# Shifted-window attention and a Fourier layer on one core: the clamp of the square sums on GpSimd, and the second normalisation written back to PSUM

## The chip, the cores and the metric

The kernel runs on one NeuronCore of a Trainium2 chip. A core has TensorE (matrix products, results in PSUM), VectorE, ScalarE (functions such as exp, log, gelu), GpSimd, and SyncE, which here only issues transfers. Each engine runs its own list of instructions in order; they are tied together by semaphores that an instruction raises when it is done and on which others wait. In the profile the engines are PE, DVE, ACT, POOL and SP; PEld is TensorE's weight load, and a name with a q is the engine's sequencer. The metric is the device time of one execution in microseconds (us).

## The reference

The input is an image batch x of shape (8, 256, 256, 64), float32. Two layers follow one another.

Layer 0 is a shifted-window transformer block. The image is cut into windows of 4x4 positions (a shift by 8 in both directions maps windows to windows). In each window, q, k and v are projections of x, with 4 heads of 16 channels:

```
qn = q / max(norm(q), 1e-12)          # likewise kn
attn = softmax(qn @ kn.T * scale + bias + mask)
x = x + layernorm(proj(attn @ v)) * g1 + b1
x = x + layernorm(fc2(gelu(fc1(x)))) * g2 + b2
```

The norms are over the 16 channels of a head; this is where the square sums and their clamp come from: max(sum of squares, 1e-24) is the square of the clamped norm. The layer norms are over the 64 channels.

Layer 1 subtracts a moving average of 25 along one axis, mixes the first 128 Fourier modes with complex matrices, one per channel, and adds the average back. It is linear and is done here as one 256x256 matrix per channel.

## The kernel before, in words

There are three stages. A short one (to about 262 us) forms constants and the 64 channel matrices. The long one, to about 6770 us, is layer 0. The last one, the Fourier layer, multiplies by the channel matrices and writes the output; it contains none of the code that is changed.

The long stage works on 512 groups. A group is 4 image rows over the full width: 64 windows, 1024 positions, laid out as 128 partitions (2 halves of the image's width x 64 channels) x 512 columns, or, turned, as 128 positions x 8 slots x channels. It is a software pipeline written out by hand: in every step each engine does one piece of work for groups of different age. In the code a group d steps old is called `i`d: `project_qk(i1)` is the projection of the group that came in one step ago, `gain2(i10)` the end of the second layer norm of the group that came in ten steps ago. The order of the calls at the end of each `step` is the engine's order. 16 steps are written out ahead of the loop and 10 behind it. The loop of TensorE unrolls 2 steps, ScalarE's 4, those of VectorE, GpSimd and SyncE 8. `need(engine, semaphore, group)` makes the engine wait for that group's piece; `before(g)` is the group that came in one step earlier.

The orders of one step, with the lines of the profile's rows:

- VectorE: regroup_x i1 (L855), normed1 i8 (L918), add1 i8 (L927), turn_prob i5 (L912), normed2 i10 (L933), gain2 i10 (L939), sum_squares i2 (L861), clamp i2 (L867), bias i4 (L884), maximum i4 (L893), turn_k i3 (L873), turn_q i3 (L879), qk_out i1 (L840), v_out i1 (L849), sum_prob i4 (L899), invert i4 (L906).
- TensorE: first_layer i9 in two halves (L595), weighted i6 (L551), scores i4 (L531), turn_x i0 (L492), project i7 (L563), second_layer i9 in two halves (L607), project_qk i1 (L502), project_v i1 (L512), variances i7 and i9 (L579, L583).
- ScalarE: keep_o i6 (L698), gelu i9 (L730), square1 i7 (L704), gelu i9 (L730), keep_x i0 (L674), a table load (L737), square2 i9 (L710), log_norm i2 (L679), root_norm i2 (L686), exponent i4 (L692), log_norms i7, i9 (L716), root_norms (L724), a table load (L744).
- GpSimd: divide i5 (L1042), square i2 (L997), expand_v i5 (L1004, two instructions), add2 i10 (L1053), shift i4 (L1036), scale_norm i2 (L1012), norm_k i2 (L1018), norm_q i2 (L1027).
- SyncE issues the transfers: store of y (L377), load of x (L341), copies of x and x1 (L346, L351), swap of halves (L364), spread_p (L358), spread_k (L371). spread_p and spread_k are four transfers each into `rows`, which TensorE's L551 and L531 read.

PSUM has eight banks of 128x512 float32. MA (banks 0, 1) and MB (2, 3) serve the projections and the first layer by turns, so that L595 waits until L840 has copied MA out. Banks 4 and 5 serve the scores (SB) and weighted sums (PV), the variances (VV) and the turned input (XT) by turns. D1 (bank 6) holds the attention's projection, H2 (bank 7) the second layer's output. normed1 writes its result back into D1; normed2 writes its result to a buffer in SBUF, `dn2`.

The clamp's chain: GpSimd squares (square), VectorE sums 16 at a time to 128x64 (sum_squares, into `ss`) and clamps (into `ssc`), ScalarE takes the log and from it the inverse root, GpSimd multiplies q and k by it.

Of the kernel before, what the change touches and what calls it, by code (L numbers as in the profile page):

```python
# [83 lines left out]
def swin_then_fourier(nc, x, qkv_wt, qkv_b, v_b, proj_wt, proj_b, logit_scale, cpb_w1t, cpb_b1, cpb_w2t,  # L84
# [11 lines left out]
    with ExitStack() as ctx:  # L96
# [11 lines left out]
        def carve(cols):  # L108
            a = used[0]
            used[0] += cols  # L110
            assert used[0] <= 2 * T * C
            return arena[:, a:a + cols]
# [41 lines left out]
        pT = carve(512)  # L154
        vexp = carve(1024).rearrange("p (s h e d) -> p s h e d", s=SLOTS, h=HEADS, e=2)
        oT = [carve(512) for _ in range(2)]
        sq1, sq1x, sq2, dn2, yg = (carve(512) for _ in range(5))
        x1T, x1r = [carve(512) for _ in range(2)], [carve(512) for _ in range(4)]
        l12, r12 = (carve(1024).rearrange("p (k n) -> p k n", k=2) for _ in range(2))
        ystripe = [sb(f"ystripe{i}", ROWS * HALF)[:, :].rearrange("p (r n) -> p r n", r=ROWS)  # L160
# [61 lines left out]
        def there(g):  # L222

            return not isinstance(g.base, int) or 0 <= g.base + g.off < G

        def need(eng, s, g, per=1):

            if there(g):
                assert isinstance(g.base, int) or PEEL + g.off >= 0
                eng.wait_ge(s, g.base * per + (g.off + 1) * per)  # L230
# [13 lines left out]
        def settled(eng):  # L244

            eng.sem_inc(passed, 1)

        def before(g, n=1):
            return Group(g.base, g.off - n)
# [176 lines left out]
        def _(pe):  # L426
# [57 lines left out]
            def step(s, k):  # L484
# [114 lines left out]
                def second_layer(g, kk, done):  # L599
                    if there(g):  # L600
                        if kk == 0:
                            need(pe, gelu0, g)
                            need(pe, dn2_sb, before(g))
                        else:
                            need(pe, gelu1, g)
                        for a in range(2):
                            ins = mm(H2[a * C:a * C + C, :], w2[:, kk, :], hT[kk][:, a, :],  # L607
                                     start=(kk == 0), stop=(kk == 1), tile_position=(0, a * C))
                        ins.then_inc(done, 1)
# [163 lines left out]
        def _(dve):  # L773
# [59 lines left out]
            def step(s, k):  # L833
# [24 lines left out]
                def sum_squares(g):  # L858
                    if there(g):
                        need(dve, squared, g)  # L860
                        dve.tensor_reduce(ss, sq.rearrange("p (n d) -> p n d", d=HD), AX.X, ALU.add).then_inc(summed, 1)  # L861

                def clamp(g):
                    if there(g):
                        need(dve, summed, g)
                        need(dve, logged, before(g, 2))
                        ts(ssc[ring(g, 2)], ss, 1e-24, None, ALU.max).then_inc(clamped, 1)  # L867

                def turn_k(g):
                    if there(g):  # L870
# [58 lines left out]
                def normed2(g):  # L929
                    if there(g):  # L930
                        need_norms(dve, r12_sb, i8, i10)
                        need(dve, yg_sb, before(g))
                        stt(dn2, H2, be2, r12[:, 1, :], ALU.add, ALU.mult).then_inc(dn2_sb, 1)  # L933

                def gain2(g):
                    if there(g):
                        need(dve, dn2_sb, g)
                        need(dve, y_sb, before(g))
                        ts(yg, dn2, g2, o12, ALU.mult, ALU.add).then_inc(yg_sb, 1)  # L939

                regroup_x(i1)
                normed1(i8)
# [2 lines left out]
                normed2(i10)  # L945
                gain2(i10)
                sum_squares(i2)
                clamp(i2)
                bias(i4)
                maximum(i4)  # L950
                turn_k(i3)
# [24 lines left out]
        @block.gpsimd  # L976
        def _(pool):
            tt = pool.tensor_tensor
            pool.memset(ident, 0.0).then_inc(made_id, 1)
            pool.wait_ge(made_id, 1)  # L980
            pool.affine_select(out=ident, in_=ident, compare_op=ALU.not_equal, fill=1.0, base=0,
                               pattern=[[-1, P]], channel_multiplier=1).then_inc(made_id, 1)
            pool.memset(qe, 0.0).then_inc(made_id, 1)
            pool.memset(rows[:, :], 0.0).then_inc(made_id, 1)
            pool.wait_ge(made_id, 4)
            pool.wait_ge(consts, consts_in)
            pool.wait_ge(set_up, 15)

            def step(s, k):
                i0, i1, i2, i3, i4, i5, i6, i7, i8, i9, i10, i11 = ago(s, k)  # L990

                def square(g):
                    if there(g):
                        need(pool, qk_sb, g)
                        need(pool, summed, before(g))
                        q = qk[ring(g, 2)].rearrange("p w s n -> p (w s n)")
                        tt(sq, q, q, ALU.mult).then_inc(squared, 1)  # L997

                def expand_v(g):
                    if there(g):  # L1000
                        need(pool, vb_sb, g)
                        need(pool, pv_ps, before(g))
                        for e, done in ((0, v0_sb), (1, v1_sb)):
                            tt(vexp.rearrange("p s h e d -> p (s h) e d")[:, :, e, :],  # L1004
                               vb[ring(g, 4)].rearrange("p (n d) -> p n d", d=HD),
                               par[:, e:e + 1].unsqueeze(2).to_broadcast([P, 32, HD]), ALU.mult).then_inc(done, 1)

                def scale_norm(g):
                    if there(g):
                        need(pool, rooted, g)  # L1010
                        r = rn[ring(g, 2)][:, 0]
                        tt(r, r, scale.unsqueeze(1).to_broadcast([P, SLOTS, HEADS]), ALU.mult).then_inc(scaled, 1)  # L1012

                def norm_k(g):
                    if there(g):
                        need(pool, rooted, g)
                        need(pool, kT_sb, before(g))
                        tt(kn.rearrange("p (n d) -> p n d", d=HD),  # L1018
                           qk[ring(g, 2)][:, 1].rearrange("p s (h d) -> p (s h) d", d=HD),
                           rn[ring(g, 2)][:, 1].rearrange("p s h -> p (s h)").unsqueeze(2).to_broadcast([P, 32, HD]),  # L1020
                           ALU.mult).then_inc(kn_sb, 1)

                def norm_q(g):
                    if there(g):
                        need(pool, scaled, g)
                        need(pool, qT_sb, before(g))
                        tt(bass.AP(tensor=qe.tensor, offset=qe.offset, ap=[qe.ap[0], [64, 16], [48, 2], [1, HD]]),  # L1027
                           qk[ring(g, 2)][:, 0].rearrange("p s (q h d) -> p (s q) h d", q=2, h=2),
                           rn[ring(g, 2)][:, 0].rearrange("p s (q h) -> p (s q) h", q=2).unsqueeze(3).to_broadcast([P, 16, 2, HD]),
                           ALU.mult).then_inc(qe_sb, 1)  # L1030

                def shift(g):
                    if there(g):
                        need(pool, maxed, g)
                        pr = prob[ring(g, 2)].rearrange("p (n m e) -> p n m e", m=N, e=2)
                        tt(pr, pr, mx.rearrange("p (n e) -> p n e", e=2).unsqueeze(2).to_broadcast([P, N, N, 2]), ALU.subtract).then_inc(shifted, 1)  # L1036

                def divide(g):
                    if there(g):
                        need(pool, prob_rec, g)  # L1040
                        pr = prob[ring(g, 2)].rearrange("p (n m e) -> p n m e", m=N, e=2)
                        tt(pr, pr, rs.rearrange("p (n e) -> p n e", e=2).unsqueeze(2).to_broadcast([P, N, N, 2]), ALU.mult).then_inc(probs, 1)  # L1042

                def add2(g):
                    if there(g):
                        need(pool, yg_sb, g)
                        need_slot(pool, x1r_in, g, 4)
                        r = ring(g, 8)
                        if r % 2 == 0:
                            if there(before(g, 8)):  # L1050
                                pool.wait_ge(y_out[r // 2], g.base * 4 + (g.off - r) * 4)
                        v = "p (x r j e) -> p x r e j"
                        tt(ystripe[r // GPS][:, r % GPS * WIN:(r % GPS + 1) * WIN, :].rearrange("p r (x e j) -> p x r e j", x=N, j=WIN),  # L1053
                           yg.rearrange(v, r=WIN, j=WIN, e=2), x1r[ring(g, 4)].rearrange(v, r=WIN, j=WIN, e=2),
                           ALU.add).then_inc(y_sb, 1)

                divide(i5)
                square(i2)
                expand_v(i5)
                add2(i10)  # L1060
                shift(i4)
                scale_norm(i2)
                norm_k(i2)
                norm_q(i2)

            over_groups(pool, step, 8)
# [37 lines left out]
```

## Time and profile before

| | us |
|---|---|
| median of 3 runs | 7964.86 (7961.18 to 7968.6) |
| the profiled execution's own time | 7957.41 |
| its span in the profile | 7955.6 |
| mean granted clock of TensorE | 0.979 of full |

Over the span, TensorE is busy for 6613.9 us, VectorE for 6520.1, ScalarE for 5628.4 and GpSimd for 5096.5. Busy shares are means over three stages. In the timeline's rows a bracket at the end of a row gives how long the engine had stood idle before this instruction and which instruction released it. Instructions of one engine can overlap a little in the rows, since they are pipelined. Times that are called start to start are the differences of two start times.

### The profile page before, as it was taken

How to read it: one execution, taken by the hardware profiler on the slowest of the kernel's cores; microseconds unless marked ns; L12 is line 12 of the kernel's file. 1: busy time of each engine (PE TensorE's matmuls, PEld its weight loads, DVE VectorE, ACT ScalarE, POOL GpSimd, SP SyncE). 2: the span in 40 equal slices, each digit the busy share in tenths (PEclk: the TensorE clock that was granted, in tenths of full speed). 3: DMA queues.
4: the chain of work that ended last, by engine and by line, in shares of the span. 5: the costliest groups of instructions: out<-in, count | busy, mean ns of one | idle time of the engine just before them, and what ended most of it. 6: DMA issues, size and time to landing. Idle time of an engine off the chain costs nothing.

```text
span 7955.6 us, 278088 instructions
## 1 busy us (share of the span) xinstructions
PE 6613.9 (83%) x105272; PEld 4133.5 (52%) x105272; DVE 6520.1 (82%) x8543; ACT 5628.4 (71%) x7004; POOL 5096.5 (64%) x4616
## 2 busy tenths in 40 slices
PE   8788888888888888888888888888888887787786
PEld 5544444444444444444444444444444444676675
DVE  1599999999999999999999999999999997222221
ACT  1488888888888888888888888888888888222221
POOL 0477777777777777777777777777777776000000
PEclk9899999999999999999999999999999999898898
DMA  2355555555555555555555555555555554999999
GB/s 98 112 148 147 146 145 145 146 147 146 146 146 146 146 146 146 145 145 146 147 147 146 147 146 146 147 146 146 144 145 147 147 146 124 331 332 354 342 332 338
DMA packets 1486082, 1370.67 MB, mean 172 GB/s; under 512 B 670097, under 2 KB 1080081, under 8 KB 1481875
## 3 DMA queue, kind: packets, MB, share of 16 engines
q1 hardware_dynamic: 1481412, 1235.63, 56.7%
q10 hardware_dynamic: 4608, 134.22, 4.0%
q8 instruction: 38, 0.62, 0.0%
q14 instruction: 24, 0.20, 0.0%
HBM read 412.97 MB, written 285.21 MB: 88 GB/s over the span
## 4 chain that ended last, share of the span: by engine, by line
DVE 49%; issue 29%; PE 14%; DMA 4%; DVEq 2%; ACT 0%; SPq 0%; POOL 0%; ACTq 0%; POOLq 0%
PE ps L632 10%; DVE arena L861 8%; DVE arena L879 8%; DVE ps L918 4%; DVE arena L884 4%; DVE arena L849 4%; DVE arena L933 4%; DVE arena L912 4%; DMA out<-arena 4%; DVE arena L899 4%; DVE arena L927 2%; DVE arena L873 2%; DVE arena L855 2%; PE ps L466 1%; DVEq L230 1%
## 5 line engine op out<-in xcount | busy, mean ns | idle before, releaser
L607 PE MATMUL ps<-mats,arena 128*64 128x512 f32 x4096 | 1083.3, 607 | 506.4 <-ACT mats L730 501.7
L595 PE MATMUL ps<-arena 64*128 64x512 f32 x4096 | 1017.5, 613 | 459.1 <-DVE arena L840 459.0
L997 POOL TENSOR_TENSOR arena<-arena 128x1024 f32<-128x1024 f32 x512 | 980.1, 1914 | 270.2 <-DVE arena L840 270.2
L730 ACT ACTIVATE mats<-ps,arena 128x1024 f32<-128x1024 f32 x1024 | 1133.1, 1107 | 0.0
L1004 POOL TENSOR_TENSOR arena<-arena 128x512 f32<-128x512 f32 x1024 | 1122.2, 1115 | 4.1 <-PE ps L551 4.1
L632 PE MATMUL ps<-rows,mats 128*128 128x256 f32 x4096 | 916.9, 388 | 234.6 <-ACT arena L751 159.4
L1036 POOL TENSOR_TENSOR arena<-arena 128x512 f32<-128x512 f32 x512 | 541.7, 1058 | 742.4 <-DVE arena L893 742.4
L963 DVE COPY arena<-ps 128x512 f32 x256 | 269.3, 1067 | 880.5 <-PE ps L632 564.0
L632 PEld LDWEIGHTS ps<-rows,mats 128*128 128x128 f32 x4096 | 796.9, 195 | 355.0 <-ACT arena L751 163.3
L595 PEld LDWEIGHTS ps<-arena 64*128 64x128 f32 x4096 | 373.5, 185 | 1129.7 <-issue 586.4
L1042 POOL TENSOR_TENSOR arena<-arena 128x512 f32<-128x512 f32 x512 | 566.8, 1107 | 544.7 <-DVE arena L906 544.7
L751 ACT ACTIVATE arena<-ps 128x512 f32 x256 | 272.1, 1085 | 873.5 <-PE ps L632 545.3
L1053 POOL TENSOR_TENSOR ystripe<-arena 128x512 f32<-128x512 f32 x512 | 776.8, 1517 | 71.3 <-DVE arena L939 71.3
L607 PEld LDWEIGHTS ps<-mats,arena 128*64 128x64 f32 x4096 | 242.9, 136 | 1052.2 <-ACT mats L730 955.3
L704 ACT ACTIVATE arena<-ps,arena 128x512 f32<-128x512 f32 x512 | 352.1, 688 | 600.5 <-PE ps L563 600.4
L502 PEld LDWEIGHTS ps<-arena 64*128 64x128 f32 x8192 | 498.9, 188 | 411.4 <-ACT arena L674 406.6
L716 ACT ACTIVATE arena<-ps,arena 128x1024 f32<-128x1024 f32 (+1 forms) x514 | 570.6, 1110 | 163.7 <-PE ps L583 158.3
L551 PEld LDWEIGHTS ps<-rows,arena 128*32 128x32 f32 x32768 | 481.8, 110 | 390.5 <-issue 390.5
L737 ACT ACT_TABLE_LOAD x522 | 669.7, 1283 | 9.1
L744 ACT ACT_TABLE_LOAD x522 | 669.7, 1283 | 9.1
L531 PE MATMUL ps<-rows,arena 128*32 128x64 f32 x32768 | 617.7, 226 | 26.5 <-DMA rows<-arena 21.1
L861 DVE TENSOR_REDUCE arena<-arena 128x64 f32<-128x1024 f32 x512 | 617.7, 1206 | 8.9 <-POOL arena L997 8.9
(94 smaller groups left out, 15274.2 us busy)
## 6 DMA issues: line engine op xcount, KB each, us to landing
arena<-arena SPq DMA_DIRECT2D x1024, 256.0 KB, 2.7
rows<-arena SPq DMA_DIRECT2D x4096, 64.0 KB, 2.0
arena<-in_x SPq DMA_DIRECT2D x1024, 128.0 KB, 2.8
arena<-arena SPq DMA_DIRECT2D x1024, 128.0 KB, 2.3
y<-ystripe SPq DMA_DIRECT2D x512, 256.0 KB, 3.3
mats<-mix SPq DMA_DIRECT2D x512, 256.0 KB, 3.4
rows<-y SPq DMA_DIRECT2D x512, 256.0 KB, 4.1
out<-arena ACTq DMA_DIRECT2D x32, 4096.0 KB, 27.2
```

The lines of the kernel that those rows point to most:

```text
L531: ins = mm(sv[32 * p:32 * p + 32, q, a, :, :, e], qT[:, a * 4 + p, q, e:64:2], kTx[:, :, a * 4 + p, q, e:32:2], start=True, stop=True, til ...
L595: ins = mm(M[:, a, :], w1[a * C:a * C + C, kk * P:(kk + 1) * P], x1T[ring(g, 2)][a * C:a * C + C, :], start=True, stop=True, tile_position ...
L607: ins = mm(H2[a * C:a * C + C, :], w2[:, kk, :], hT[kk][:, a, :], start=(kk == 0), stop=(kk == 1), tile_position=(0, a * C))
L632: ins = mm(ps[:, j, k * T:(k + 1) * T], amat[j][:, r * T + k * P:r * T + (k + 1) * P], xch[j][:, r * T:(r + 1) * T], start=(r == 0), stop= ...
L730: f(hT[kk], M, ACT.Gelu, bias=b1[:, kk:kk + 1]).then_inc(done, 1)
L737: act.preload_act_table_set(EXP_SET)
L744: act.preload_act_table_set(GELU_SET)
L861: dve.tensor_reduce(ss, sq.rearrange("p (n d) -> p n d", d=HD), AX.X, ALU.add).then_inc(summed, 1)
L879: dve.transpose(qT.rearrange("p s q n -> p (s q n)"), qe).then_inc(qT_sb, 1)
L997: tt(sq, q, q, ALU.mult).then_inc(squared, 1)
L1004: tt(vexp.rearrange("p s h e d -> p (s h) e d")[:, :, e, :], vb[ring(g, 4)].rearrange("p (n d) -> p n d", d=HD), par[:, e:e + 1].unsqueeze ...
L1053: tt(ystripe[r // GPS][:, r % GPS * WIN:(r % GPS + 1) * WIN, :].rearrange("p r (x e j) -> p x r e j", x=N, j=WIN), yg.rearrange(v, r=WIN, ...
```

## The change

The clamp becomes an instruction of GpSimd's list, between expand_v and add2, and it waits there for the sum. sum_squares, on VectorE, now also waits for the previous group's clamp, because `ss` has one buffer that GpSimd reads. normed2 writes its result in place into H2, in PSUM, instead of into `dn2`, and gain2 reads it there; `dn2` is gone. So H2 is in use until gain2 is done, and TensorE's second_layer waits for the previous group's gain2 (`yg_sb`) where it waited for its normed2 (`dn2_sb`). The order of TensorE's work is unchanged.

```diff
-        sq1, sq1x, sq2, dn2, yg = (carve(512) for _ in range(5))
+        sq1, sq1x, sq2, yg = (carve(512) for _ in range(4))
@@ second_layer, TensorE
                         if kk == 0:
                             need(pe, gelu0, g)
-                            need(pe, dn2_sb, before(g))
+                            need(pe, yg_sb, before(g))
@@ sum_squares and clamp, VectorE
                         need(dve, squared, g)
+                        need(dve, clamped, before(g))
                         dve.tensor_reduce(ss, sq.rearrange("p (n d) -> p n d", d=HD), AX.X, ALU.add).then_inc(summed, 1)
-
-                def clamp(g):
-                    if there(g):
-                        need(dve, summed, g)
-                        need(dve, logged, before(g, 2))
-                        ts(ssc[ring(g, 2)], ss, 1e-24, None, ALU.max).then_inc(clamped, 1)
@@ normed2 and gain2, VectorE
-                        stt(dn2, H2, be2, r12[:, 1, :], ALU.add, ALU.mult).then_inc(dn2_sb, 1)
+                        stt(H2, H2, be2, r12[:, 1, :], ALU.add, ALU.mult).then_inc(dn2_sb, 1)
-                        ts(yg, dn2, g2, o12, ALU.mult, ALU.add).then_inc(yg_sb, 1)
+                        ts(yg, H2, g2, o12, ALU.mult, ALU.add).then_inc(yg_sb, 1)
@@ VectorE's order
                 sum_squares(i2)
-                clamp(i2)
                 bias(i4)
@@ GpSimd
+                def clamp(g):
+                    if there(g):
+                        need(pool, summed, g)
+                        need(pool, logged, before(g, 2))
+                        settled(pool)
+                        pool.tensor_scalar(ssc[ring(g, 2)], ss, 1e-24, None, ALU.max).then_inc(clamped, 1)
@@ GpSimd's order
                 expand_v(i5)
+                clamp(i2)
                 add2(i10)
```

`settled(engine)` raises a semaphore on which nobody waits.

## Rows read from the trace of the kernel before

**Rows 1.** The page: busy us by engine, and the chain's shares by engine.
```profile
PE 6613.9 (83%) x105272; PEld 4133.5 (52%) x105272; DVE 6520.1 (82%) x8543; ACT 5628.4 (71%) x7004; POOL 5096.5 (64%) x4616
...
DVE 49%; issue 29%; PE 14%; DMA 4%; DVEq 2%; ACT 0%; SPq 0%; POOL 0%; ACTq 0%; POOLq 0%
```
**Rows 2.** Line L840: count, durations (ns), first and last start (us).
```profile
L840 DVE TENSOR_TENSOR arena<-ps,arena x490: 1180/1185/1191, 445.3 to 6591.8; 128x1024 f32<-128x1024 f32 x164
```
**Rows 3.** Timeline, VectorE, one step: start us, us, engine line op out<-in, count.
```profile
3904.71 0.75 DVE L918 SCALAR_TENSOR_TENSOR ps<-ps,arena 128x512 f32<-128x512 f32 x1
3905.75 0.75 DVE L927 SCALAR_TENSOR_TENSOR arena<-ps,arena 128x512 f32<-128x512 f32 x1 [0.29 <-DVE ps L918]
...
3907.05 0.71 DVE L933 SCALAR_TENSOR_TENSOR arena<-ps,arena 128x512 f32<-128x512 f32 x1
3907.79 1.06 DVE L939 TENSOR_SCALAR arena<-arena 128x512 f32<-128x512 f32 x1
3908.77 1.21 DVE L861 TENSOR_REDUCE arena<-arena 128x64 f32<-128x1024 f32 x1
3910.01 1.27 DVE L867 TENSOR_SCALAR arena<-arena 128x64 f32<-128x64 f32 x1
3911.20 0.68 DVE L884 TENSOR_TENSOR arena<-ps,arena 128x512 f32<-128x512 f32 x1
...
3914.26 1.19 DVE L840 TENSOR_TENSOR arena<-ps,arena 128x1024 f32<-128x1024 f32 x1
```
**Rows 4.** L867 while the pipeline fills; L849 in the step; L855, 3000 to 5000.
```profile
287.70 0.20 DVE L867 TENSOR_SCALAR arena<-arena 128x64 f32<-128x64 f32 x1
...
3902.87 0.67 DVE L849 COPY arena<-ps 128x512 f32<-128x512 f32 x1
...
L855 DVE COPY arena<-arena x159: 360/363/1236, 3012.0 to 4998.1; 128x512 f32<-128x512 f32 x159
```
**Rows 5.** Timeline, ScalarE and TensorE, from one L716 to the next.
```profile
3902.26 1.11 ACT L716 ACTIVATE arena<-ps,arena 128x1024 f32<-128x1024 f32 x1 [0.37 <-PE ps L583]
...
3903.00 1.99 PE L595 MATMUL ps<-arena 64*128 64x512 f32 x8 [0.81 <-DVE arena L840]
...
3904.48 1.28 ACT L744 ACT_TABLE_LOAD   x1
...
3906.16 0.60 ACT L698 ACTIVATE arena<-ps 128x512 f32<-128x512 f32 x1 [0.40 <-PE ps L551]
...
3907.03 0.66 PE L492 MATMUL ps<-arena 128*128 128x128 f32 x4
...
3910.58 1.08 PE L607 MATMUL ps<-mats,arena 128*64 128x512 f32 x4 [1.02 <-ACT mats L730]
...
3914.02 0.60 PE L583 MATMUL ps<-arena 64*64 64x512 f32 x2
...
3914.68 1.11 ACT L716 ACTIVATE arena<-ps,arena 128x1024 f32<-128x1024 f32 x1 [0.28 <-PE ps L583]
```
**Rows 6.** Timeline, GpSimd, the same step.
```profile
3904.60 1.11 POOL L1042 TENSOR_TENSOR arena<-arena 128x512 f32<-128x512 f32 x1 [1.11 <-DVE arena L906]
...
3907.53 2.21 POOL L1004 TENSOR_TENSOR arena<-arena 128x512 f32<-128x512 f32 x2
...
3909.71 1.52 POOL L1053 TENSOR_TENSOR ystripe<-arena 128x512 f32<-128x512 f32 x1
...
3912.68 1.06 POOL L1036 TENSOR_TENSOR arena<-arena 128x512 f32<-128x512 f32 x1 [1.45 <-DVE arena L893]
...
3913.75 0.25 POOL L1012 TENSOR_TENSOR arena<-arena 128x32 f32<-128x32 f32 x1
```
**Rows 7.** Timeline, spread_k and scores; the page: issues, KB, us to landing.
```profile
3913.27 2.49 SPq L371 DMA_DIRECT2D rows<-arena  x4
...
3918.50 1.21 PE L531 MATMUL ps<-rows,arena 128*32 128x64 f32 x64
...
rows<-arena SPq DMA_DIRECT2D x4096, 64.0 KB, 2.0
```

## The prediction

> **What bounds the kernel now.** I read the page's busy shares first [rows 1]: TensorE 83%, VectorE 82%, ScalarE 71%, GpSimd 64%. These average three stages. Then the shares of the chain of waits [rows 1]: VectorE is on it for 49% of the whole span, TensorE 14%, and "issue" 29%. The last stage has none of the changed code, so VectorE's share in the window-attention stage is larger still. That stage repeats one step per group of windows. The first VectorE instruction of a projection that is copied out, L840, comes 490 times from 445.3 to 6591.8 us [rows 2]: (6591.8 - 445.3) / 489 = 12.57 us a step. The timeline of one step shows VectorE with almost no hole: from L918 to L840 each instruction begins as the one before ends [rows 3]. The other engines wait on it: TensorE's L595 stands 0.81 us for L840 [rows 5], GpSimd's L1036 1.45 us and L1042 1.11 us for VectorE results [rows 6]. So VectorE is the bound, at one step per 12.57 us, and what leaves its queue is worth its full time until another loop gets longer.
>
> **Part 1, the clamp leaves VectorE.** L867 handles only 128x64 values and yet takes 1.27 us; L884 starts 1.19 us after it starts [rows 3]. During the filling of the pipeline, with GpSimd idle, the same instruction took 0.20 us [rows 4]. In the step it begins at 3910.01 while GpSimd's add L1053 runs from 3909.71 to 3911.23 [rows 6], and ends at 3911.28, just after that. So about 1.0 of its 1.27 us is waiting for GpSimd, and all of it goes: VectorE saves 1.19 us a step.
> The Trainium skill (SBUF - State Buffer, Who interferes with whom) says why: tensor_scalar in a two-port mode and GpSimd share a port pair under an exclusive lock. By that rule this trace's 0.20 against 1.27 us is one mechanism, and it agrees.
>
> **Part 2, gain2 reads PSUM.** L939, SBUF to SBUF, takes 1.06 us; L861 starts 0.98 us after it [rows 3]. From PSUM, the nearest row is the copy L849, 128x512, 0.67 us [rows 4], though GpSimd works beside it. Going by that row gain2 holds VectorE for 0.65 us: 0.33 less. The uncertain thing is the wait for normed2's result when it lies in PSUM: L918 writes PSUM and L927, which reads it (and has four more waits), starts with a 0.29 us hole [rows 3]; L939 now starts 0.03 us after L933 ends. So the hand-over costs 0.03 to 0.32 us; I take 0.05, since gain2 has two waits only. Normed2 itself grows from 0.71 to L918's 0.75 us [rows 3], +0.04. Net saving 0.27 (0 to 0.3).
> A rule speaks against this part. The row first: SBUF-to-SBUF copy L855 needs 0.36 us where nothing blocks it, and 1.24 us at worst [rows 4]. The Trainium skill (VectorE: DVE Perf Modes, Why PSUM operands drop a tier) says a PSUM operand loses the two-port mode, so fp32 falls to 1x. By it alone gain2 would go from 0.36 to 0.67 and the part would lose 0.3 us; but the row that counts is the 1.06 us of L939, which begins while GpSimd's L1004 runs [rows 6], and against that it wins.
>
> **VectorE's own loop afterwards:** 12.57 - 1.19 - 0.27 = 11.1 us. It has to be asked what is late next.
>
> **The loop through ScalarE and TensorE** [rows 5], counted from L716 (variances' log) to the next L716. L716 to the table load L744: 2.22. The load, 1.28. Then L698 (keep_o) at once, now held back 0.40 us more by TensorE's L551, which will be 0.8 us earlier once L595 no longer waits: 0.02 + 0.60. Hand-over 0.05, sum 4.17, and TensorE's L492 starts (it needs the bank that L698 reads). L492 to the second pair of L607 3.55 (project, its square and a gelu lie between): 7.72. L607 to the end of L583: 3914.62 - 3910.58 = 4.04, to L716 0.06. Sum 11.82 us. This is longer than VectorE's 11.1, so it takes over: the saving of 1.46 is cut to 0.75.
> Does VectorE keep pace inside that loop? L716 to L918 2.45, L918 to L939 3.08 + 0.04, gain2 0.65, L861 1.24, L884 to L840 3.06, L840 1.19, hand-over 0.05: L595 could start 11.76 after L716. L595 to L492 is 4.03 (3903.00 to 3907.03), and L492 starts at 11.82 + 4.17 = 15.99 anyway, so L595 has until 11.96: hidden by 0.2; at the high end of the PSUM hand-over (+0.27) 0.07 us a step late.
>
> **Part 3, TensorE waits for gain2, not normed2.** Behind that wait in TensorE's queue stand both pairs of L607, then the projections and the variances, so all of the step's second half. gain2 ends 2.45 + 3.08 + 0.04 + 0.67 = 6.24 after L716, up to 6.5. The first pair then runs 1.1 us to 7.35 (7.6 at most); the second pair waits for the gelu until 7.72 in any case. Cost nothing; the cover is 0.1 to 0.4 us thick.
>
> **Part 4, the clamp on GpSimd,** between expand_v and add2. It waits for L861: 2.45 + 3.08 + 0.04 + 0.65 + 1.21, hand-over 0.05 = 7.5 after L716. Queued behind it are add2, shift, and the three normalisations; ScalarE's log, its exponential and VectorE's transposes wait for those. The trace has no such GpSimd instruction; the two nearest rows are L1012 (128x32, 0.25 us) and L1053 (128x512, 1.52 us) [rows 6]. I take 0.3, nearest to L1012 by size. Add2 then ends 7.5 + 0.3 + 1.55 = 9.35 and L1036 starts there, 2.47 before the next L716 at 11.82. Today it starts 2.00 before it (3912.68, 3914.68) [rows 5, 6]. So nothing on the path moves; a clamp up to 0.3 + 0.47 = 0.77 us is covered. sum_squares' new wait for the previous clamp is met a step ago. GpSimd's idle of 2.5 us a step pays for the 0.3.
>
> **SyncE's queue:** its order stays. spread_k (L371) starts 1.41 before L716, takes 2.49 for four issues, and each needs 2.0 us to land [rows 7]: the last lands 2.5 to 3.1 after L716, depending on whether landing counts from the start or the end of the 0.6 us issue. L531 now starts 3.82 after L716 [rows 5, 7] and would start 0.8 earlier, at 3.0. Even at 3.1 L492 follows 1.1 later, at 4.2 against 4.17. Nothing, with no reserve.
>
> **Sum.** At the end of VectorE's loop, once in eight steps, L855 comes late and is blocked by GpSimd (1.24 us at most against 0.36 [rows 4]): at most 0.88 / 8 = 0.11 us a step, part of today's 12.57; later some 0.04, since VectorE then has slack before L918. Another 0.04 for TensorE's and ScalarE's loop ends, which are hidden today. New step 11.9 us, gain 0.67 us, times some 500 full steps = 335 us. Profiled execution 7957.4 us (span 7955.6 + 1.8), so 7622; the median of the runs lies 7.5 us higher: 7630 us. Filling, draining and the last stage stay.
>
> **Rivals.**
> (A) The forecast: ScalarE and TensorE take over at 11.6 to 12.15 us a step, 7495 to 7770 us. 68%.
> (B) VectorE stays the bound at 11.1 us because the loop above has slack that its rows hide: 7965 - 1.47 x 500 = 7230 us. The rows speak against it: every link but L698 is tight. 4%.
> (C) spread_k's transfers become the bound. The same work in 5% less time; if landing takes 0.5 us more, L531 starts at 3.4, L492 at 4.5, and a step is 12.2 us: 7780 us. For it: no reserve. Against it: in the step of the rows L531 comes 0.7 to 1.3 us after the last landing, and 0.8 of that is what goes. 20%.
> (D) Slower: GpSimd's clamp is dear. From 0.77 us on, each 0.1 us of it pushes add2, shift, exponential and so L716 by as much; from 0.77 + 0.75 = 1.5 us a step is longer than today's. At 2.0 us a step would be 13.05 and the kernel 7965 + 240 = 8205 us. For it: no row shows this form on GpSimd, and L1053 at 1.52 stands just on the edge. Against it: 64 values, and L1012's 0.25 us. 6%.
> (E) The gain is eaten whole, or the edits leave VectorE's holes where the instructions were: 7965. 2%.
>
> **Numbers.** A measurement of this kernel can tell about 0.2%, 16 us. Faster: A, B and nearly all of C, 0.91; same: E and the edge of C, 0.03; slower: D, 0.06. The time is A's, 7630; the range, 7500 to 7800, takes in A and the nearer half of C.
>
> **What would show it.** L867 gone from VectorE, 64-value instructions of about 0.3 us on GpSimd; gain2 at 0.67 us and no longer dependent on GpSimd; VectorE with a hole before L918 (released by ScalarE's L724); TensorE's wait before L595 gone or under 0.1 us; L698 starting right behind the table load; steps of 11.9 us. I am wrong if L607's first pair waits so long for gain2 that its second pair moves, if L531 waits for a transfer, or if the GpSimd clamp is over 0.8 us.

## The result, and the profile after

The changed kernel takes 7619.25 us (median of 4 runs, 7617.64 to 7621.8), the kernel before 7963.02 us beside it: a ratio of 0.9568 (0.9551 to 0.9584), 344 us less. The forecast was 7630 us. The profiled execution has a span of 7617.0 us, 338.6 less than the one before.

The page of the changed kernel, busy us and the chain's shares by engine, against [rows 1]; then L840's count and first and last start in the stretch to 6100 us, against [rows 2]:

```profile
PE 6695.2 (88%) x105272; PEld 4078.5 (54%) x105272; DVE 5889.3 (77%) x8031; ACT 5593.4 (73%) x7004; POOL 5235.2 (69%) x5128
...
PE 52%; ACT 24%; issue 16%; DMA 4%; ACTq 2%; SPq 1%; POOL 0%; DVE 0%; POOLq 0%; DVEq 0%
```
```profile
L840 DVE TENSOR_TENSOR arena<-ps,arena x476: 1180/1186/1225, 442.0 to 6090.7; 128x1024 f32<-128x1024 f32 x159
```

VectorE's share of the chain fell from 49% to 0%, and TensorE with ScalarE has 76%. A step takes (6090.7 - 442.0) / 475 = 11.89 us instead of 12.57. Times the 500 steps of the sum, that is 340 us. From the first of all 512 L840 to the last it is 339.3 us less (274.6 to 6679.4 us before, 274.4 to 6339.9 after), and the span is 338.6 less: nothing else in the kernel moved.

The timeline of one step, ScalarE and TensorE, from one L716 to the next, as in [rows 5]:

```profile
3904.57 1.99 PE L595 MATMUL ps<-arena 64*128 64x512 f32 x8
3904.71 1.11 ACT L716 ACTIVATE arena<-ps,arena 128x1024 f32<-128x1024 f32 x1 [0.61 <-PE ps L583]
...
3906.93 1.28 ACT L744 ACT_TABLE_LOAD   x1
...
3908.23 0.60 ACT L698 ACTIVATE arena<-ps 128x512 f32<-128x512 f32 x1
...
3908.97 0.63 PE L492 MATMUL ps<-arena 128*128 128x128 f32 x4 [0.28 <-ACT arena L698]
...
3910.91 1.08 PE L607 MATMUL ps<-mats,arena 128*64 128x512 f32 x4 [0.30 <-DVE arena L934]
...
3912.49 1.08 PE L607 MATMUL ps<-mats,arena 128*64 128x512 f32 x4 [0.50 <-ACT mats L730]
...
3915.92 0.60 PE L583 MATMUL ps<-arena 64*64 64x512 f32 x2
...
3916.59 1.12 ACT L716 ACTIVATE arena<-ps,arena 128x1024 f32<-128x1024 f32 x1 [0.48 <-PE ps L583]
```

See the brackets. keep_o (L698) starts at the table load's end with no idle before it, where it waited 0.40 us; TensorE's L492 now waits for it. L595, which stood 0.81 us for L840, has no wait any more and starts right behind the variances. The first pair of L607 has the new wait for gain2 (L934).

VectorE and GpSimd in the same step. The line numbers have moved: L913, L934, L862, L879 are the L918, L939, L861, L884 of [rows 3], and L1054, L1037 are the L1053, L1036 of [rows 6]. L998 is the clamp.

```profile
3906.95 0.76 DVE L913 SCALAR_TENSOR_TENSOR ps<-ps,arena 128x512 f32<-128x512 f32 x1 [0.72 <-ACT arena L724]
...
3910.05 0.81 DVE L934 TENSOR_SCALAR arena<-ps,arena 128x512 f32<-128x512 f32 x1
...
3910.77 1.21 DVE L862 TENSOR_REDUCE arena<-arena 128x64 f32<-128x1024 f32 x1
...
3911.90 0.68 DVE L879 TENSOR_TENSOR arena<-ps,arena 128x512 f32<-128x512 f32 x1
...
3912.20 0.37 POOL L998 TENSOR_SCALAR arena<-arena 128x64 f32<-128x64 f32 x1 [1.21 <-DVE arena L862]
...
3912.53 1.52 POOL L1054 TENSOR_TENSOR ystripe<-arena 128x512 f32<-128x512 f32 x1
...
3914.01 1.06 POOL L1037 TENSOR_TENSOR arena<-arena 128x512 f32<-128x512 f32 x1
```

VectorE has a hole of 0.72 us before normed1: it waits for ScalarE. GpSimd's idle has moved from before divide and shift (1.11 and 1.45 us) to before the clamp (1.21 us), with 0.59 us before scale_norm.

### The profile page after: what moved, and what is told of

Read it like the earlier page. It is cut to its first block, busy times and chain, and to the rows that moved or that the text cites. A ratio compares the mean times of both kernels' runs of the same rounds, so it can differ in the third digit from the quotient of the medians.

```text
span 7617.0 us, 278601 instructions
## 1 busy us (share of the span) xinstructions
PE 6695.2 (88%) x105272; PEld 4078.5 (54%) x105272; DVE 5889.3 (77%) x8031; ACT 5593.4 (73%) x7004; POOL 5235.2 (69%) x5128
## 4 chain that ended last, share of the span: by engine, by line
PE 52%; ACT 24%; issue 16%; DMA 4%; ACTq 2%; SPq 1%; POOL 0%; DVE 0%; POOLq 0%; DVEq 0%
PE ps L632 11%; ACT mats L730 7%; ACT arena L716 7%; PE ps L502 7%; PE ps L607 7%; PE ps L563 7%; PE ps L579 7%; PE ps L512 6%; ACT L744 5%; PE ps L492 4%; ACT arena L698 4%; DMA out<-arena 4%; PE ps L466 1%; ACTq L230 1%; PE ps L457 1%
## 5 line engine op out<-in xcount | busy, mean ns | idle before, releaser
L607 PE MATMUL ps<-mats,arena 128*64 128x512 f32 x4096 | 1104.7, 616 | 410.8 <-ACT mats L730 234.2
L1005 POOL TENSOR_TENSOR arena<-arena 128x512 f32<-128x512 f32 x1024 | 1042.6, 1038 | 3.4 <-PE ps L551 3.3
L595 PE MATMUL ps<-arena 64*128 64x512 f32 x4096 | 1018.4, 615 | 0.5 <-DVE arena L840 0.4
L1054 POOL TENSOR_TENSOR ystripe<-arena 128x512 f32<-128x512 f32 x512 | 782.1, 1527 | 41.6 <-DVE arena L934 41.6
L607 PEld LDWEIGHTS ps<-mats,arena 128*64 128x64 f32 x4096 | 211.3, 135 | 1085.1 <-ACT mats L730 696.0
L716 ACT ACTIVATE arena<-ps,arena 128x1024 f32<-128x1024 f32 (+1 forms) x514 | 571.2, 1111 | 263.3 <-PE ps L583 260.0
L502 PEld LDWEIGHTS ps<-arena 64*128 64x128 f32 x8192 | 500.0, 188 | 411.8 <-ACT arena L674 407.4
L595 PEld LDWEIGHTS ps<-arena 64*128 64x128 f32 x4096 | 356.8, 186 | 656.8 <-issue 360.1
L704 ACT ACTIVATE arena<-ps,arena 128x512 f32<-128x512 f32 x512 | 351.9, 687 | 479.0 <-PE ps L563 479.0
L913 DVE SCALAR_TENSOR_TENSOR ps<-ps,arena 128x512 f32<-128x512 f32 x512 | 388.5, 759 | 336.6 <-ACT arena L724 336.6
L531 PE MATMUL ps<-rows,arena 128*32 128x64 f32 x32768 | 617.6, 226 | 27.4 <-DMA rows<-arena 18.7
L1043 POOL TENSOR_TENSOR arena<-arena 128x512 f32<-128x512 f32 x512 | 631.6, 1234 | 10.6 <-DVE arena L901 9.8
L862 DVE TENSOR_REDUCE arena<-arena 128x64 f32<-128x1024 f32 x512 | 618.8, 1209 | 9.5 <-POOL arena L991 9.5
```

Of the source, the lines that this page charges most:

```text
L502: ins = mm(MA[:, a, p * P:(p + 1) * P], xT[ring(g, 2)][a * C:a * C + C, p * P:(p + 1) * P], wqkv[a * C:a * C + C, 0:2 * C], start=True, st ...
L595: ins = mm(M[:, a, :], w1[a * C:a * C + C, kk * P:(kk + 1) * P], x1T[ring(g, 2)][a * C:a * C + C, :], start=True, stop=True, tile_position ...
L716: f(l12[:, k, :], VV[:, k, :], ACT.Ln, bias=eps).then_inc(l12_sb, 1)
L1005: tt(vexp.rearrange("p s h e d -> p (s h) e d")[:, :, e, :], vb[ring(g, 4)].rearrange("p (n d) -> p n d", d=HD), par[:, e:e + 1].unsqueeze ...
```

## The experiments

All were timed beside the kernel before, whose medians were 7959.6 to 7965.3 us. A step's length is worked out from L840's first and last start, as above.

**1. Gain2 alone.** The clamp stays on VectorE.

```diff
-                        stt(dn2, H2, be2, ...)
+                        stt(H2, H2, be2, ...)
-                        ts(yg, dn2, g2, o12, ...)
+                        ts(yg, H2, g2, o12, ...)
-                            need(pe, dn2_sb, before(g))
+                            need(pe, yg_sb, before(g))
```

> Only the second half of the change: normed2 in place in PSUM, gain2 from PSUM, TensorE waits for gain2; the clamp stays on VectorE. Additive theory: gain2 holds VectorE for 0.72 us as in the changed kernel instead of 0.98, VectorE stays the bound, 0.26 us x 500 steps = 130 us less, 7835 us. Port theory: in the step before, GpSimd's add2 starts 5.19 us after invert ends and the clamp 5.49 us after it; a clamp that comes 0.26 us earlier, at 5.23, still finds add2 running and is released at the same moment, so the saving turns into waiting: 7960 us, the clamp's row about 1.5 us long. If the clamp came before add2 it would take 0.2 us and the kernel would drop towards 7650 us.

7877.8 us, ratio 0.9893 (0.9877 to 0.991): 83 us less, a step of 12.40 us. That is neither of the two numbers expected, and the clamp's row is 1.32 us at the median, 1.27 before, where the port theory had 1.5. GpSimd and VectorE in a step of it:

```profile
3920.05 1.11 POOL L1042 TENSOR_TENSOR arena<-arena 128x512 f32<-128x512 f32 x1 [1.13 <-DVE arena L906]
...
3922.98 2.03 POOL L1004 TENSOR_TENSOR arena<-arena 128x512 f32<-128x512 f32 x2
...
3924.98 1.52 POOL L1053 TENSOR_TENSOR ystripe<-arena 128x512 f32<-128x512 f32 x1
3925.23 1.32 DVE L867 TENSOR_SCALAR arena<-arena 128x64 f32<-128x64 f32 x1
...
3926.46 0.68 DVE L884 TENSOR_TENSOR arena<-ps,arena 128x512 f32<-128x512 f32 x1
```

The clamp still arrives during add2 and is let in at its end: add2's start to bias (L884) is 1.48 us, before it was 1.49. So the clamp's end is still tied to add2's, as the port theory said; between 3000 and 5000 us each clamp starts while add2 runs, before (159 times) and here (161). But expand_v (L1004, two instructions) takes 2.03 instead of 2.21 us. Before, gain2 ran from 3907.79 to 3908.85 across the point where the second of the two begins; now it reads PSUM and is 0.81 us long whatever GpSimd does. L1042 to L1053 is 4.93 instead of 5.11 us [rows 6], and this 0.18 is what the step is shorter by, 0.17 us. The step before was therefore bound by a loop through both engines: L1042, square, expand_v, to add2's start 5.11; the blocked clamp, to bias, 1.49; VectorE to L1042 again, 5.90. That is 12.50 us, the length of seven of eight steps.

**2. The clamp alone** on GpSimd; normed2 and gain2 as before the change.

> Only the first half: the clamp on GpSimd; normed2 writes SBUF, gain2 reads SBUF, TensorE waits for normed2. My theory: the step is bound by the loop of ScalarE and TensorE (11.87 us in the changed kernel), so part 2 gives nothing once the clamp is away: gain2 blocked by expand_v at 1.0 to 1.3 us, VectorE's hole of 0.6 us before normed1 pays for it, 7620 to 7670 us. Rival (both halves count): VectorE is 0.26 us a step slower and the kernel with it, 7750 us.

7630.7 us, ratio 0.9584 (0.9568 to 0.96), a step of 11.91 us: 12 us above the changed kernel, intervals overlapping. The second half of the change is worth 83 us alone; beside the first it is worth 12 us, which is not clear of the noise. In the timeline gain2 is blocked again, and VectorE's hole pays:

```profile
3909.22 0.76 DVE L913 SCALAR_TENSOR_TENSOR ps<-ps,arena 128x512 f32<-128x512 f32 x1 [0.74 <-ACT arena L724]
...
3912.30 1.23 DVE L934 TENSOR_SCALAR arena<-arena 128x512 f32<-128x512 f32 x1
```

VectorE's steps alternate here: L840 starts at 3905.17, 3917.64, 3928.86 and 3941.55 us, 12.5, 11.2 and 12.7 apart, and gain2 takes 1.23, 0.55 and 1.37 us in them. ScalarE's L716 comes evenly all the same, at 3906.98, 3918.86 and 3930.74, 11.88 apart as in the changed kernel. So the loop of ScalarE and TensorE sets the mean, but with little to spare: TensorE waits for L840 in 207 of the 476 steps between 440 and 6100 us, 55.2 us in all, and VectorE has 18% of the chain.

**3. Another kind of instruction at the clamp's place.**

```diff
-                        ts(ssc[ring(g, 2)], ss, 1e-24, None, ALU.max)
+                        dve.tensor_reduce(ssc[ring(g, 2)], ss.rearrange("p (n d) -> p n d", d=1), AX.X, ALU.max)
```

> The kernel before with one edit: VectorE's clamp is replaced by a tensor_reduce over an axis of one element, which only copies the 64 sums (the clamp itself is left out). It stays at the same place of VectorE's list. Port theory (1.0 of the clamp's 1.27 us is waiting for GpSimd's add2 because of the kind of instruction): the row falls to 0.15 to 0.25 us, VectorE's own loop to 11.5 us, the ScalarE-TensorE loop takes over at 11.9, 7620 to 7680 us. Rival (a small instruction at that place takes 1.2 us whatever it is, for its waits): 7960 us.

7694.8 us, ratio 0.9665 (0.9649 to 0.9681). L867's durations (ns, least, median, most) between 3000 and 5000 us, then a row of the waits (us in total, times, longest):

```profile
L867 DVE TENSOR_REDUCE arena<-arena x166: 219/220/223, 3007.7 to 4993.1; 128x64 f32<-128x64 f32 x166
```
```profile
PE ps L595 <- DVE arena L840: 43.8, 83, 0.7
```

0.22 us, always, beside the same add2 (all 166 start while it runs): the 1.27 us were the price of the kind of instruction, not of its place, its waits or its size. The Trainium skill (SBUF — State Buffer, Who interferes with whom) says tensor_reduce never contends for the shared pair on trn2; these rows agree. The time is 15 us above the range I gave: a step is 12.04 us. Here too VectorE's steps alternate: L840 starts at 3900.87, 3913.55, 3925.00 and 3937.68 us, 12.7, 11.45 and 12.7 apart. The short one is VectorE's own loop with hardly a wait; gain2, which still reads SBUF, takes between 0.57 and 1.38 us. In one step of two (83 of 166) L840 comes late for TensorE and L595 waits; in the changed kernel it waits 0.4 us for L840 in the whole execution.

**4. ScalarE's table load behind keep_o,** in the changed kernel.

```diff
                 keep_o(i6)
+                act.preload_act_table_set(GELU_SET)
                 gelu(i9, 0, MA, fc1a_ps, fc2a_ps, gelu0)
...
                 root_norms(i7, i9)
-                act.preload_act_table_set(GELU_SET)
```

> The changed kernel with ScalarE's gelu table load moved behind keep_o. My theory: keep_o, which starts right behind the load, is on the loop that bounds the step; it starts 0.5 us earlier, TensorE's turn_x 0.35 us earlier, but the load then delays the first gelu and square1 follows it at once, so that 0.13 us a step are gained: 7555 us (7530 to 7590). Rival (VectorE is still the bound): 7619 us, no change.

7580.0 us, ratio 0.9524 (0.9508 to 0.954): 39 us less than the changed kernel, a step of 11.81 us. The loop is the one named, and the time lies in the range given, at 39 of the 64 us expected. It gives 0.09 instead of 0.13 us a step: the load now stands between keep_o and the gelu, and the gelu's end is at once the start of square1 (L704, no idle before it):

```profile
3906.63 0.60 ACT L698 ACTIVATE arena<-ps 128x512 f32<-128x512 f32 x1 [0.74 <-PE ps L551]
...
3907.25 1.28 ACT L733 ACT_TABLE_LOAD   x1
...
3908.54 1.11 ACT L730 ACTIVATE mats<-ps,arena 128x1024 f32<-128x1024 f32 x1
...
3909.55 0.68 ACT L704 ACTIVATE arena<-ps,arena 128x512 f32<-128x512 f32 x1
```

**5 and 6. How dear may the clamp be on GpSimd?** One and three more clamps ahead of the real one, in the changed kernel.

```diff
+                        for w in spare:
+                            pool.tensor_scalar(w, ss, 1e-24, None, ALU.max)
                         pool.tensor_scalar(ssc[ring(g, 2)], ss, 1e-24, None, ALU.max).then_inc(clamped, 1)
```

> The changed kernel with a second clamp on GpSimd ahead of the real one, into spare memory: 0.33 us more per step start to start. Prediction's reckoning: covered up to 0.77 us in all, so 7619 us. The same by the rows of the changed kernel.

> The changed kernel with three more clamps on GpSimd ahead of the real one, 1.0 us more, 1.36 in all. Prediction's reckoning (from 0.77 us on, one to one): 0.59 us x 500 = 295 us more, 7910 us. By the rows of the changed kernel there is a second piece of cover, the 0.49 us that ScalarE stands idle before the variances' log behind the exponential, besides the 0.39 us between shift's end and the exponential: 0.12 us x 500 = 60 us more, 7680 us.

Two clamps: 7623.5 us, ratio 0.9577 (0.9561 to 0.9593), no difference. Four: 7644.0 us, ratio 0.9605 (0.9589 to 0.9621), 25 us more, nearer to the 60 than to the 295. GpSimd has 21% of the chain now, where it had 0%. The exponential (here L693) now waits for shift, and the variances' log (L717) follows it without idle; both pieces of cover are used up:

```profile
3917.25 0.63 ACT L693 ACTIVATE arena<-arena 128x512 f32<-128x512 f32 x1 [0.70 <-POOL arena L1040]
3917.79 1.10 ACT L717 ACTIVATE arena<-ps,arena 128x1024 f32<-128x1024 f32 x1
```

**7. gain2 earlier,** before turn_prob in VectorE's list.

```diff
-                turn_prob(i5)
                 normed2(i10)
                 gain2(i10)
+                turn_prob(i5)
```

> The changed kernel with VectorE doing normed2 and gain2 before turn_prob, so gain2 is done 0.7 us earlier and TensorE's 0.3 us wait for it (first pair of second_layer) goes. My theory: the second pair waits for the gelu anyway, no change, 7619 us within 0.2%. Rival (the new wait costs its full length): 0.35 us x 500 = 175 us less, 7445 us.

7623.4 us, ratio 0.9578 (0.9562 to 0.9594): no difference. TensorE's waits before L607, 3000 to 5000 us, first of the changed kernel, then of this one, where gain2 is gone from them:

```profile
PE ps L607 <- ACT mats L730: 76.4, 168, 0.7
...
PE ps L607 <- DVE arena L934: 54.3, 147, 0.5
```
```profile
PE ps L607 <- ACT mats L730: 166.8, 168, 1.0
```

The wait only changed its name: 0.32 us a step for gain2 and 0.45 for the gelu became 0.99 for the gelu.

**8. More work on GpSimd, in the kernel before.**

```diff
                 expand_v(i5)
+                if there(i10):
+                    need(pool, y_sb, before(i10))
+                    settled(pool)
+                    pool.tensor_scalar(spare, ident, 1e-24, None, ALU.max)
                 add2(i10)
```

> The kernel before with work added: GpSimd does one more tensor_scalar, 128x128 from the identity into spare memory, between expand_v and add2 (0.4 to 0.5 us). Loop theory, from the 0.18 us a step that the gain2-only kernel won: the step before is bound by a loop through GpSimd and the port, L1042 to add2 5.11 us, add2's start to bias 1.49, bias to L840 3.06, L840 to L1042 2.84. The clamp arrives 0.30 us after add2's start and is let in when the running GpSimd instruction ends. With the short instruction there instead of add2 it is let in after 0.45 us and not after 1.52: VectorE gains 0.9 us a step, add2 starts some 0.6 us later, in time for shift. More work on GpSimd makes the kernel faster: 7700 us (7650 to 7780), the clamp's row 0.3 to 0.6 us. Rival 1 (VectorE alone sets the step, GpSimd's extra work is hidden): 7960 us. Rival 2 (GpSimd is on the loop and its work simply adds): 0.4 x 500 = 200 us more, 8160 us.

7820.5 us, ratio 0.9823 (0.9807 to 0.984): 145 us faster with more to do, which neither rival allows. Of the 260 us that I expected it is about half. In the timeline of a step where it works as thought the short instruction (L1064) is running when the clamp (L868) arrives:

```profile
3916.28 0.52 POOL L1064 TENSOR_SCALAR arena<-arena 128x128 f32<-128x128 f32 x1
...
3916.57 0.28 DVE L868 TENSOR_SCALAR arena<-arena 128x64 f32<-128x64 f32 x1
3916.68 0.68 DVE L885 TENSOR_TENSOR arena<-ps,arena 128x512 f32<-128x512 f32 x1
```

The next step is another. This is VectorE from the L841 (the L840 of before) at the end of the step above to the one after, then the clamp's durations between 3000 and 5000 us:

```profile
3919.75 1.19 DVE L841 TENSOR_TENSOR arena<-ps,arena 128x1024 f32<-128x1024 f32 x1
...
3923.58 0.76 DVE L919 SCALAR_TENSOR_TENSOR ps<-ps,arena 128x512 f32<-128x512 f32 x1 [0.74 <-ACT arena L725]
...
3926.67 1.23 DVE L940 TENSOR_SCALAR arena<-arena 128x512 f32<-128x512 f32 x1
...
3929.05 0.76 DVE L868 TENSOR_SCALAR arena<-arena 128x64 f32<-128x64 f32 x1
...
3932.80 1.19 DVE L841 TENSOR_TENSOR arena<-ps,arena 128x1024 f32<-128x1024 f32 x1
```
```profile
L868 DVE TENSOR_SCALAR arena<-arena x163: 272/278/770, 3007.4 to 4997.6; 128x64 f32<-128x64 f32 x163
```

The steps alternate, 11.43 us (3908.32 to 3919.75) and 13.05 us here, and so do the clamps: 82 take about 0.28 us, 81 wait for add2's end and take 0.67 us or more. This is what took back the other half. After a short step VectorE is ahead of ScalarE and waits for it (L919, 0.74 us); it then meets GpSimd later in its list, so that gain2 takes 1.23 instead of 1.06 us and the clamp arrives behind the short instruction, during add2.

**9. The projection between the halves of second_layer,** on top of experiment 4.

```diff
                 second_layer(i9, 0, fc2a_ps)
-                second_layer(i9, 1, fc2b_ps)
                 project_qk(i1)
+                second_layer(i9, 1, fc2b_ps)
```

> The kernel with keep_o ahead of the gelu table load (e4), and TensorE doing project_qk between the two halves of second_layer. There TensorE stands 0.3 us for the second gelu behind a 0.6 us wait for gain2. Theory: the loop is now gelu, second half, projections, variances; with 1.0 us of projection moved before the second half TensorE's wait for the gelu goes, and the variances come 0.13 us earlier until they wait for square2 behind ScalarE's other table load: 7515 us (7490 to 7560). Rival (ScalarE, 10.9 of its 11.75 us busy, or VectorE's feed of 11.7 us holds the step): 7580 us.

7574.7 us, ratio 0.9512 (0.9496 to 0.9528), against 7580.0: no difference, a miss. The wait for the gelu went as meant (10.9 us in 2000 instead of 67.3). By the chain, what holds most steps now is the other wait before L607, the one that this change brought in:

```profile
PE ps L607 <- DVE arena L934: 100.3, 147, 0.9
...
ACT arena L674 <- DMA arena<-arena: 24.9, 67, 1.4
```

It was as long in experiment 4 (97.0 us), but there the gelu covered it. VectorE has 17% of the chain here and 3% there, with normed1, turn_prob, normed2 and gain2: the variances' log and inverse root, these four and add1, and the second half of TensorE's step form a loop. From L716 at 3940.34 us to L607 at 3946.64 to the next L716 at 3952.00 it takes 11.66 us. In some steps a transfer adds to it: keep_x (L674) waits for one in 67 of 170 steps, 24.9 us, against 41 times and 13.5 us in experiment 4.

## Why the prediction was right, and where not

**The loop that takes over.** Right, by its own sum: L716 to L716 was worked out as 11.82 us and is 11.88 in the step shown; link by link 2.22, 1.30, 0.74 to L492 (0.65 forecast), 3.52 to the second pair of L607 (3.55), 4.10 to the next L716 (4.10). The mean step is 11.89 us against 11.9. Experiment 4 moves one link of that loop, and the time moves; experiments 2, 5 and 7 change VectorE, GpSimd and TensorE's new wait off the loop, and it stays. The bounds of (A) in us are 15 too high by its own rule: 11.6 and 12.15 us a step give 7480 and 7755.

**What bound the kernel before.** Half right, and this is the step of the prediction that failed, without showing in the total. I took VectorE for the bound because its row has no holes, and said that what leaves its queue is worth its full time. But a VectorE instruction that waits for the port is shown as busy. Experiment 1 took 0.25 us out of gain2, but the clamp was still let in only at add2's end; the 0.17 us a step that came are those by which GpSimd reached add2 sooner. Experiment 8 adds half a microsecond of work to GpSimd, and the kernel is 1.8% faster. The bound was the loop through both engines. For part 1 this makes no difference, since the clamp was the blocked instruction itself; experiment 3, which leaves it on VectorE in a kind that doesn't need the port, gets 77% of the change's gain (266 of 344 us), with the maximum itself left out.

**Part 2.** Sized nearly right for VectorE, and worth nearly nothing to the kernel. gain2 from PSUM takes 0.81 us, not L849's 0.67, and 0.72 start to start instead of 0.65; the hand-over after normed2 is 0.04 us (0.05 taken). From normed2's start to sum_squares' start it is 1.48 us where it was 1.72 [rows 3], so VectorE saves 0.24 us a step, 0.27 forecast; of this the kernel sees 12 us, within the noise (experiment 2).

**Part 3.** Right: the first pair starts 6.20 us after L716 (6.24 forecast) and waits 0.30 us, up to 0.5 in other steps; the second pair is let go by the gelu at 7.78 (7.72), and experiment 7 shows that nothing is lost. It is no reserve for further savings, as experiment 9 shows.

**Part 4.** The clamp takes 0.37 us (0.3). The cover was reckoned too thin: 0.47 us and then one to one; experiment 6 puts 1.0 us more there for 25 us, 0.05 a step. I had overlooked that ScalarE stands idle between the exponential and the next log. The slower rival (D) had its threshold at 1.5 us. By an estimate from experiment 6 (1.36 us of clamps cost 0.05 us a step, and from there one to one up to the 0.68 us that the change gains) it would have been some 2.0.

**SyncE's transfers** (C) were in time, as the chain says: spread_k's L531 starts 2.77 us after L716 (3907.48), earlier than the 3.0 reckoned with, and between 3000 and 5000 us no wait for a transfer stands before it.

## What to carry to other kernels

An engine with a full row isn't the bound by that alone: look for an instruction whose duration is out of proportion to its size (here 1.27 us for 64 values a partition, 0.20 when the other engine is idle) and ends with another engine's; its engine may be waiting, and the other engine may be on the loop too. Before pricing a saving, add up the next longest loop with hand-overs; here it cut 1.46 us to 0.68. And of two savings on one engine, the one that suffices to reach the next loop takes nearly all: of 344 us the clamp alone brings some 330.

## What the runs showed of the hardware that I had not expected

- VectorE's tensor_scalar on 128x512 from PSUM takes 0.810 us (809 to 812 ns, 168 times), the copy of the same size 0.675.
- GpSimd's tensor_scalar on 128x64 takes 0.366 us (365 to 367 ns), on 128x128 0.52 where nothing disturbs it.
- Between two GpSimd instructions a waiting VectorE instruction is let in: expand_v's pair takes 2.03 us alone and 2.21 us with gain2 in the middle. So one more, short GpSimd instruction can make the kernel faster (experiment 8).
- A VectorE instruction that is held up so is recorded as busy: the 1.27 us clamp of before shows no idle, and VectorE was busy for 1928 of the 2000 us from 3000 to 5000.
